# A graph network's second gather stage: edge tiles gathered for a pair of node tiles

## The reference, cut to what matters

```python
summed = segment_sum(x[src], dst, num_segments=n)
deg = segment_sum(ones_like(src), dst, num_segments=n)
agg = summed / maximum(deg, 1.0)[:, None]
out = concatenate([x, agg], axis=-1) @ weight
out = out / norm(out, axis=-1, keepdims=True)
return out + bias
```

## Time and profile before

| | us |
|---|---|
| Median of 3 runs (6247.11 to 6253.21) | 6248.97 |
| The profiled execution, its own time | 6250.95 |
| its span, first to last instruction | 6249.3 |
| TensorE busy | 4928.5 |
| GpSimd busy | 4157.3 |
| VectorE busy | 4061.6 |
| ScalarE busy | 1780.0 |

### The profile page before, as it was taken

One profiled execution on the slowest core, in us unless ns is written; L12 is line 12 of the kernel. 1 busy time (PEld: TensorE's weight loads), 2 busy tenths in 40 slices (PEclk: granted clock), 3 DMA queues, 4 the chain that ended last, 5 costly groups with the idle time before them and its releaser, 6 DMA issues. The chain is left out here.

```text
span 6249.3 us, 102386 instructions
## 1 busy us (share of the span) xinstructions
PE 4928.5 (79%) x33929; PEld 4410.6 (71%) x33930; DVE 4061.6 (65%) x10205; ACT 1780.0 (28%) x4090; POOL 4157.3 (67%) x4057
## 2 busy tenths in 40 slices
PE   4427999999999999999995666666666666666887
PEld 3326999999999999999994555555555555555887
DVE  5526988898888889888984343443443443435776
ACT  2302444444444444444441000000000000003554
POOL 1347777777777777777754777777777777771323
PEclk9658999999999999999997888878878877887999
DMA  6655555555555565555543555555555555553221
GB/s 183 167 145 144 150 147 149 152 148 148 149 151 149 147 150 150 147 148 154 147 106 91 133 139 137 133 143 134 134 142 134 134 142 134 139 132 106 82 63 51
DMA packets 610386, 848.90 MB, mean 136 GB/s; under 512 B 251280, under 2 KB 424418, under 8 KB 609276
## 3 DMA queue, kind: packets, MB, share of 16 engines
q0 software_dynamic: 181728, 505.88, 30.9%
q1 hardware_dynamic: 384538, 275.47, 17.5%
q10 hardware_dynamic: 43650, 61.62, 2.9%
HBM read 728.24 MB, written 116.75 MB: 135 GB/s over the span
## 5 line engine op out<-in xcount | busy, mean ns | idle before, releaser
L1234 POOL DMA_INDIRECT m_ring<-tab_a,m_src x1764 | 1989.0, 1128 | 672.3 <-issue 504.0
L1856 POOL DMA_INDIRECT eb_rows<-tab_b,eb_src x1764 | 1740.5, 987 | 541.1 <-issue 537.0
L2100 PE MATMUL eb_acc<-eb_rows,eb_S 128*128 128x257 f32 x3528 | 1076.2, 473 | 439.8 <-DMA eb_rows<-tab_b,eb_src 438.6
L2100 PEld LDWEIGHTS eb_acc<-eb_rows,eb_S 128*128 128x128 f32 x3528 | 842.3, 244 | 635.7 <-DMA eb_rows<-tab_b,eb_src 468.6
L1515 PE MATMUL m_acc<-m_V,m_S 128*128 128x264 f32 x3528 | 862.1, 390 | 0.0
L1515 PEld LDWEIGHTS m_acc<-m_V,m_S 128*128 128x128 f32 x3528 | 646.9, 192 | 93.4
L1909 DVE TENSOR_TENSOR eb_sum<-eb_acc,eb_sum 128x257 f32<-128x257 f32 x98 | 41.8, 426 | 1009.1 <-PE eb_acc L2100 1009.1
L1636 ACT ACTIVATE mh_high<-m_ps,bn_b,bn_s 128x256 fp32r<-128x256 f32 x784 | 441.4, 563 | 747.9 <-PE m_ps L537 744.8
L525 DVE TENSOR_TENSOR mh_low<-mh_full,mh_high 128x512 fp32r<-128x512 f32 x784 | 544.5, 695 | 107.7 <-ACT mh_full L1636 61.4
L1625 ACT ACTIVATE mh_full<-m_ps,bn_b,bn_s 128x256 f32<-128x256 f32 x784 | 400.6, 563 | 674.6 <-DVE mh_low L525 355.1
L1309 DVE TENSOR_TENSOR m_V<-m_ring,m_V 128x1280 f32<-128x1280 f32 (+1 forms) x392 | 532.7, 1359 | 13.4
(11 more groups left out here) (388 smaller groups left out, 10221.1 us busy)
## 6 DMA issues: line engine op xcount, KB each, us to landing
m_dstb<-dst_p SPq DMA_DIRECT2D x196, 320.0 KB
m_dstb<-dst_p SPq DMA_DIRECT2D x196, 256.0 KB
m_ring<-tab_a,m_src POOLq DMA_INDIRECT x1764
eb_rows<-tab_b,eb_src POOLq DMA_INDIRECT x1764, 2.8
routed<-rXR ACTq DMA_DIRECT2D x49, 513.0 KB, 8.7
xw_stage<-in_L_ffn_w_dram ACTq DMA_DIRECT2D x16, 1024.0 KB, 8.4
over<-b_blank SPq DMA_DIRECT2D x9, 1452.0 KB, 15.4
mOV<-over SPq DMA_DIRECT2D x49, 264.0 KB, 4.8
```

The source lines that it names most:

```text
L1234: gp.indirect_dma_start(out=ring[:, j, :], out_offset=None, in_=scratch["tab_a"], in_offset=bass.IndirectOffsetOnAxis(ap=src[:, j:j + 1], ...
L1856: gp.indirect_dma_start(out=rows_[q.par][j][:, t, 0:D], out_offset=None, in_=scratch["tab_b"], in_offset=bass.IndirectOffsetOnAxis(ap=src_ ...
L2100: last_i = nc.tensor.matmul(ps_acc[j][:, 0:NR], S[q.par][j][:, t, :], rows_[q.par][j][:, t, :], start=t == 0, stop=t == WT - 1)
```

## The change

A pair of node tiles now has one window of 35 edge tiles (`PW`), from the first edge of its first tile, in place of two of 18. They are gathered once, in chunks of 9, 9, 9 and 8. As an edge of any of the 35 may go to either node tile, each is multiplied with two masks, and summed into both accumulators: 70 products for a pair where there were 36, and 70 masks. The masks stand in four buffers, one for each chunk, each with both node tiles' masks; the buffer of chunk `c` is filled for the next pair when this pair's chunk `c` is summed. Both `collect` stand behind all four builds and wait for the pair's last sum. The overflow's entries for this stage are worked out for pairs (`PAIR0`, `OVER1`). In `attend_mix` the node numbers, two buffers by turns before, are one that is raised by 128 each tile.

TensorE's new order is `turn_mean`, `project`, `sum_up(q, 0)`, `turn`, `router`, `sum_up(q, 1)`, `position`, `sum_up(q, 2)`, `record`, `sum_up(q, 3)`.

```diff
+PAIR0 = LIST0 + P + 1
+OVER1 = PAIR0 + VT
+PW = 35
+CHUNKS = (9, 9, 9, 8)
+CHUNK0 = (0, 9, 18, 27)
...
+            two = row[:, 0:P].rearrange("x (n t) -> x n t", t=2)
+            step(nc.vector.tensor_tensor(pair_start[:, :, 0:1], two[:, :, 0:1], two[:, :, 1:2], MIN))
+            step(nc.vector.tensor_copy(pair_start[:, :, 1:2], pair_start[:, :, 0:1]))
+            step(nc.vector.tensor_copy(k["visits"][:, PAIR0:PAIR0 + VT], pair_start[:, :, :].rearrange("x n t -> x (n t)")[:, 0:VT]))
+            step(nc.vector.tensor_tensor(pair_cnt[:, :, :], row[:, P:2 * P].rearrange("x (n t) -> x n t", t=2), pair_start[:, :, :], SUB))
+            flat = pair_cnt[:, :, :].rearrange("x n t -> x (n t)")
+            step(nc.vector.tensor_scalar(mini[:, :], flat, 1.0 / (OT * P), 0.5 - 0.5 / (OT * P) - PW / OT, MUL, ADD))
+            step(nc.vector.tensor_scalar(k["visits"][:, OVER1:OVER1 + VT], mini[:, 0:VT], 1.0, None, MAX))
+            step(nc.vector.tensor_scalar(pair_over[:, :, :].rearrange("x n t -> x (n t)"), flat, float(PW * P), None, ALU.is_gt))
+            step(nc.vector.tensor_tensor(k["over_row"][:, :], k["over_row"][:, :], pair_over[:, :, :].rearrange("x n t -> x (n t)"), MAX))
...
-    rows_ = [[sbuf(ctx, f"eb_rows{i}{j}", [P, WT, NR]) for j in pair] for i in pair]
-    S = [[sbuf(ctx, f"eb_S{i}{j}", [P, WT, P]) for j in pair] for i in pair]
+    rows_ = [sbuf(ctx, f"eb_rows{i}", [P, PW, NR]) for i in pair]
+    S = [sbuf(ctx, f"eb_S{c}", [P, 2, CHUNKS[c], P]) for c in chunks]
...
             def stage(q):
                 if has(q, 2):
                     sp.wait_ge(summed, q.n * 4 - 4)
-                for j in pair:
-                    e0 = sp.value_load(k["visits"][0:1, bass.ds(q.n * 2 + j, 1)], min_val=0, max_val=ET * P)
-                    for to, name in ((src_s, "src_p"), (dst_s, "dst_p")):
-                        sp.dma_start(to[q.par][:, j, :], scratch[name][bass.ds(e0, WT * P)].rearrange("(p c) -> p c", c=WT))\
-                            .then_inc(staged[q.par], 16)
+                e0 = sp.value_load(k["visits"][0:1, bass.ds(q.n * 2 + PAIR0, 1)], min_val=0, max_val=ET * P)
+                for to, name in ((src_s, "src_p"), (dst_s, "dst_p")):
+                    sp.dma_start(to[q.par][:, :], scratch[name][bass.ds(e0, PW * P)].rearrange("(p c) -> p c", c=PW))\
+                        .then_inc(staged[q.par], 16)
...
             def body(q):
-                gp.wait_ge(staged[q.par], q.half * 64 + 64)
-                gather(q, 0)
-                if not has(q, 1):
-                    excess(gp, "r_pool", nothing, piece, nothing)
-                gather(q, 1)
+                gp.wait_ge(staged[q.par], q.half * 32 + 32)
+                for c in chunks:
+                    gather(q, c)
+                    if c == 1 and not has(q, 1):
+                        excess(gp, "r_pool", nothing, piece, nothing)
...
+            def build(q, c):
+
+                if c == 0:
+                    v.wait_ge(nodes_ok, q.n * 2 + 2)
+                    for j in pair:
+                        nc.vector.tensor_scalar(node_no[j][:, :], node_no[j][:, :], float(2 * P), None, ADD).then_inc(nodes_ok, 1)
+                    v.wait_ge(nodes_ok, q.n * 2 + 4)
+                    v.wait_ge(staged[q.par], q.half * 32 + 32)
+                if has(q, 1):
+                    v.wait_ge(summed, q.n * 4 + c - 3)
+                at = slice(CHUNK0[c], CHUNK0[c] + CHUNKS[c])
+                for j in pair:
+                    incident(S[c][:, j, :, :], dst_s[q.par][:, at], node_no[j], CHUNKS[c]).then_inc(S_ok, 1)
 
             def collect(q, j):
 
-                v.wait_ge(summed, q.n * 4 + 2 * (j + 1))
+                v.wait_ge(summed, q.n * 4 + 4)
...
             def body(q):
                 part = finish(q.prev()) if has(q, 1) else iter((0, 0, 0, 0))
-                if has(q, 1):
-                    collect(q.prev(), 1)
+                next(part)
                 next(part)
                 if not last(q):
                     build(q.next(), 0)
...
                 if not last(q):
                     build(q.next(), 1)
                 next(part)
-                collect(q, 0)
-                next(part)
+                if not last(q):
+                    build(q.next(), 2)
+                    build(q.next(), 3)
+                for j in pair:
+                    collect(q, j)
             groups(v, body)
-            collect(end, 1)
...
+            def sum_up(q, c):
+                pe.wait_ge(gathered[q.par][c], (q.half + 1) * (16 * CHUNKS[c]))
+                pe.wait_ge(S_ok, q.n * 8 + 2 * c + 2)
                 if c == 0 and has(q, 1):
-                    pe.wait_ge(M_ok, q.n * 2 + (j - 1))
+                    pe.wait_ge(M_ok, q.n * 2)
+                for j in pair:
+                    for x in range(CHUNKS[c]):
+                        t = CHUNK0[c] + x
+                        last_i = nc.tensor.matmul(ps_acc[j][:, 0:NR], S[c][:, j, x, :], rows_[q.par][:, t, :],
+                                                  start=t == 0, stop=t == PW - 1)
                 last_i.then_inc(summed, 1)
```

More of the change, by code:

```diff
@@ L41 @@
 NOWHERE = 1 << 14
-VT = 128
+VT = NT + 1
 WT = 18
@@ L48 @@
 LIST0 = 3 * VT
+PAIR0 = LIST0 + P + 1
[3 more added lines that the diff above has]
+CHUNK0 = (0, 9, 18, 27)
+assert sum(CHUNKS) == PW
 QUARTERS = (5, 4, 5, 4)
@@ L173, in prepare @@
     mini = sbuf(ctx, "visit_mini", [1, P])
+    pair_start, pair_cnt, pair_over = (sbuf(ctx, "visit_" + n, [1, P // 2, 2]) for n in ("pair", "pair_cnt", "pair_over"))
     ends_d = nc.dram_tensor("tile_ends", (2, RB * P), FP32, kind="Internal").ap()
@@ L1116, in attend_mix @@
     f = sbuf(ctx, "m_f", [P, big, 2 * H])
-    node_no = [sbuf(ctx, f"m_nodes{i}", [P, P]) for i in pair]
+    node_no = sbuf(ctx, "m_nodes", [P, P])
     col_i = sbuf(ctx, "m_col_i", [P, 1], I32)
-    node_col = [sbuf(ctx, f"m_col{i}", [P, 1]) for i in pair]
+    node_col = sbuf(ctx, "m_col", [P, 1])
     U = sbuf(ctx, "mU", [P, GM, NA])
@@ L1744, in mean_route @@
     staged = [s_(f"staged{i}") for i in pair]
-    gathered = [[[sem(ctx, f"r_gathered{i}{j}{c}", pool_dma=True) for c in pair] for j in pair] for i in pair]
+    gathered = [[sem(ctx, f"r_gathered{i}{c}", pool_dma=True) for c in chunks] for i in pair]
     o_fetched = sem(ctx, "r_o_fetched", pool_dma=True)
@@ L1850, in _, with gather @@
                              base=0, pattern=[[1, P]], channel_multiplier=-1).then_inc(const, 1)
[L1851 to L1858, removed]
+            gp.wait_ge(blank, 5)
+            def gather(q, c):
+                for t in range(CHUNK0[c], CHUNK0[c] + CHUNKS[c]):
+                    gp.indirect_dma_start(out=rows_[q.par][:, t, 0:D], out_offset=None, in_=scratch["tab_b"],
+                                          in_offset=bass.IndirectOffsetOnAxis(ap=src_s[q.par][:, t:t + 1], axis=0))\
+                        .then_inc(gathered[q.par][c], 16)
             def piece(r, n, w):
@@ L1881, in _ @@
             for i in pair:
-                for j in pair:
-                    nc.vector.memset(rows_[i][j][:, :, D:NR], 1.0).then_inc(blank, 1)
+                nc.vector.memset(rows_[i][:, :, D:NR], 1.0).then_inc(blank, 1)
                 nc.vector.memset(before_[i][:, :], 0.0).then_inc(blank, 1)
@@ L2005, in finish @@
                 yield
-            for j in pair:
-                build(Group(0, 0, 0), j)
+            for c in chunks:
+                build(Group(0, 0, 0), c)
             v.wait_ge(w_in, 64)
@@ L2072, in _ @@
             pe.wait_ge(lane_ok, 3)
-            pe.wait_ge(blank, 7)
+            pe.wait_ge(blank, 5)
             def before(it, n):
```

56 lines of the change are left out of this document (20 added, 36 removed).

## The result

The changed kernel takes 6344.78 us (median of 4 runs, 6343.05 to 6349.79) against 6249.89 for the one before: ratio 1.0154, 95% interval 1.014 to 1.0169. It is slower by 95 us; 171 were forecast. The profiled execution took 6349.79 us, 98.8 more than the profiled one before, with a span of 6348.1 and a mean granted clock of 0.925.

A forecast was written before the change was run, and what follows sets the result against it. The gather queue was taken to pace `mean_route`, the bound passing to TensorE's loop at 49.8 us a pair: last sum +168.9 us, tail +0.4, `prepare` +2.0, in all +171 on 6250.95, giving 6420 us; range 6282 to 6490 us.

The forecast's parts named there:

- `attend_mix`: 0, with at most 0.4 us gained: Node numbers raised by as many instructions as before, hidden by TensorE's full slices: 0, at most 0.4 us gained at the start.
- The loop of 49.8 us: TensorE's loop for a pair in `mean_route`: 47.0 us at full clock plus 2.8 for half clock, forty-eight times.
- Steps 1 to 3: From a pair's last sum through fourth build, both `collect` and the chain to the next sum: 10.2 us, some 4.5 idle.
- the clock's 2.8: Loss a pair from half clock after TensorE's idle time at the pair boundary: 2.8 us, bounds 0 and 5.1.
- Step 4: The pair's first sum on TensorE: 8.36 us, covering exactly the wait for VectorE's norms.
- Step 5: `turn`, ScalarE's copy and the router, between first and second sum: 3.6 us.
- Step 6: Two sums 16.7 us, `position` and `record` about 0.7 us, and the last sum 7.4 us.
- GpSimd's pair at 46.8 us: Gather queue in `mean_route`: 35 gathers of 1.25 us plus 3.0 us of mask bursts, so the saved gather is given back.
- `prepare`: Eight more small VectorE instructions, each waiting for the one before, at a pitch of 0.25 us: +2.0 us.
- The clock holds: Rival, chance 0.12: TensorE's loop in `mean_route` stays 47.0 us at full clock, 6286 us; GpSimd's floor 6268 us.
- The masks block GpSimd in full: Rival, chance 0.02: each mask burst holds the gathers for all of its 2.63 us, 54.3 us a pair, 6633 us.
- The gather queue stays the pace and gets shorter: Rival, chance 0.06: stretched gathers don't grow in number, TensorE's loop closes within 45.3 us, 49 gathers go, 6193 us.

## Why the prediction was right, and where it was not

The sign and the mechanism held: the bound passes from the gather queue to TensorE's loop, by the fourth build and by the clock. The time lies in the widened range of 6282 to 6490 us, but the forecast was 76 us too high, and its own range was missed (6367 to 6478 us, a loop of 48.7 to 51.0). The distance would have been larger without luck: two errors of opposite sign cancel in part.

- **"`attend_mix`: 0, with at most 0.4 us gained" failed.** It cost 24.7 us. I counted instructions and what hides them; the count was right (TensorE's row is full, 486 products a pair in both). What failed is the assumption that a product keeps its pace if its code isn't touched. The kernels with other tile sizes show it: same instructions, 25 us.
- **The loop of 49.8 us is 47.7** (mean 47.66; the pair shown takes 47.89). 48 loops are 103 us of the forecast. In its own steps, for the pair shown:
  - Steps 1 to 3 with the clock's 2.8: 13.0 forecast, 13.5 measured (4533.29 to 4546.80). The idle time was 4.34 us for 4.5. The clock took more than the 2.8: 3.0 in `project` and 0.9 in the transposes (1.95 us, 1.06 before). I had sized it by a sum that was partly over when the clock came back; here the slow stretch covers the thin work whole. What is left for the steps themselves is 9.6 for 10.2.
  - Step 4: 8.85 for 8.36 (4546.80 to 4555.65). The sum took 7.99, and TensorE then waited 0.86 us for VectorE's norms, which I had as exactly covered.
  - Step 5: 2.25 for 3.6 (4555.65 to 4557.90). The 3.6 had been read while the clock was at half before the change, from about 4532.3 (not 4532.4), so it was too slow for a loop reckoned at the full clock.
  - Step 6: 23.3 for 24.8 (4557.90 to 4581.18). **This is the term that was mis-sized most**, with step 5: 0.232 us a product instruction was 4.18 / 18, which counts the last instruction in full (0.38 us), though the next work starts beside it. From one sum's start to the next, 36 instructions take (4565.94 - 4557.90) / 36 = 0.223 us with `position` in it. `position` and `record`, which had 0.7 us of their own in the forecast, add next to nothing between these starts.
  - Without the clock's 3.9 us the pair shown would take 44.0 us, not the 47.0 of the forecast. So the full-clock loop was 3.0 us too long and the clock's price 1.1 too small.
- GpSimd's pair at 46.8 us held where it can be seen: 46.81 with half the products. That its masks cost 0.75 us a burst held in sum (3.2 us for 3.0), while the reason was finer, the rest of the mask instruction in which a gather starts. In the changed kernel itself it is less, 35 x (1.005 - 0.946) = 2.1, as the fourth burst falls into GpSimd's wait for the lists. The mean gather was to be above 1.02 us; it is 1.005, and the waits for the lists are some 1.4 us a pair for 3. These are the same slack, smaller because the loop is shorter.
- `prepare`: its eight instructions take 66.83 to 68.86, the 2.0 us forecast, and 0.6 us reached `attend_mix`. The first pair's four sums took 33.3 us from 3404.4 (3378.5, moved by the stage's later start of 25.3 and 0.6 more), where 33.9 were forecast.
- Rivals. *The clock holds* was run: TensorE's loop falls under GpSimd's, and the time is 6281.5 with the addresses' 25 us in it (some 6257 without, by subtraction), where I gave 6286 and named 6268 as the floor. *The masks block GpSimd in full*: the block is full, but it lasts for the rest of one instruction and not for the 2.63 us of a burst, at which the rival was priced; doubling the bursts cost 0.39 us a pair. The Trainium skill's page "SBUF — State Buffer", section "SBUF: two separate sides", has a VectorE instruction with two inputs in SBUF hold the shared ports for its whole length against a GpSimd one that reads SBUF, while the other blocks. The trace agrees, at every place in a burst (0.99 us left and 0.85 lost, 1.14 and 1.02, 0.15 and 0.02). The prediction had applied this to the whole burst, and so took the row, which agrees with the page, for evidence against it. *The gather queue stays the pace and gets shorter*: it stays the pace once the build is moved, and is 46.3, not 45.3.

## What to carry over

Where an edit changes the size of an on-chip tensor that is allocated ahead of others, compare the pace of stages it doesn't touch: here a tile of 32 bytes that went from between weights and features cost 25 us, over a third of what the rewritten stage lost itself. An instruction that waits for the last reader of its buffer stands at the end of the loop, however cheap; count the idle time that it makes on the bound's engine once for itself and once for the clock. A saved item on the pacing queue is worth its price only as long as that queue paces, so run the pieces apart before crediting a change with either.

## What the runs showed that I had not expected

- TensorE's products with fp32r operands keep a pace that depends on where the operands lie: 57.3 or 57.8 us for 486 products and all, at a granted clock of 1.00 in both, when the distance of two groups of tiles changes by 32 bytes (177280 and 177248). Seven kernels agree; what part of TensorE or of the memory does it, and with what period, stays open.
- A gather on GpSimd's queue that starts while VectorE makes masks is longer by what is left of that one mask instruction, less some 0.13 us (0.99 left, 0.85 lost; 1.14 left, 1.02 lost). What a burst costs is then a matter of phase.
- Work of no use pays: 36 products of zeros a pair, 4.21 us each time, in TensorE's idle time made the kernel 63 us faster than the change alone, at a granted clock of 0.98 in place of 0.89. The gather queue then sets the pace, so 63 us is not all that the clock was worth to TensorE.
